# VectorE takes the low half of the turned units ahead of a coming tile's statistics

## The reference

```python
def _layernorm(x, axis=-1, eps=1e-05):
    m = jnp.mean(x, axis=axis, keepdims=True)
    v = jnp.var(x, axis=axis, keepdims=True)
    return (x - m) / jnp.sqrt(v + eps)

# cross attention, 8 heads of 128
q = (x @ Wq).reshape(B, Tq, h, C) * SCALE
k = (context @ Wk).reshape(B, Tk, h, C) * SCALE
v = (context @ Wv).reshape(B, Tk, h, C)
attn = jax.nn.softmax(jnp.einsum('bqhc,bkhc->bhqk', q, k), axis=-1)
out = jnp.einsum('bhqk,bkhc->bqhc', attn, v).reshape(B, Tq, h * C)
return out @ Wo + bo
...
# feed-forward: a shared expert, and routed ones whose weights are truncated
out_shared = _sq_relu(xf @ Ws1) @ Ws2
logits = xf @ Wr
...
prob = jnp.trunc(prob)
...
x = x + _L0_xattn_ref(_layernorm(x, axis=-1), ...)
x = x + _L0_ffn_ref(_layernorm(x, axis=-1), ...)
```

## Time and profile before

| what | value |
|---|---|
| median of 3 runs | 117.61 us (117.22 to 117.66) |
| profiled execution | 117.36 us |
| its span, first to last instruction | 115.5 us |
| granted TensorE clock, mean | 0.993 |
| TensorE matmuls busy | 109.2 us (95%), 854 instructions |
| VectorE busy | 87.8 us (76%), 350 instructions |
| ScalarE busy | 85.5 us (74%), 348 instructions |
| GpSimd busy | 65.5 us (57%), 106 instructions |

### The profile page before, as it was taken

How to read it: one execution, slowest core, us unless ns; L and a number is a source line. 1 busy time by engine, 2 the same in 40 slices (tenths; PEclk the granted TensorE clock), 3 DMA queues, 4 the chain that set the end, 5 groups by cost and what they waited for, 6 DMA issues and landing times.

```text
span 115.5 us, 3118 instructions
## 1 busy us (share of the span) xinstructions
PE 109.2 (95%) x854; PEld 105.9 (92%) x854; DVE 87.8 (76%) x350; ACT 85.5 (74%) x348; POOL 65.5 (57%) x106
## 2 busy tenths in 40 slices
PE   6976999999999999999999999999999999989981
PEld 6974999899998989999999999999999999979970
DVE  1009888569889697797979797797979696798963
ACT  4006925997948979898988889898988889994320
POOL 2005735855372965785676578657746865469250
PEclk9999999999999999999999999999999999999997
DMA  3799999994000200040005001300500050031032
GB/s 63 252 336 357 354 355 350 346 349 160 6 6 0 91 0 3 6 146 35 0 0 182 0 0 61 121 0 0 182 0 0 0 182 3 0 124 57 38 136 98
DMA packets 11815, 12.70 MB, mean 110 GB/s; under 512 B 1056, under 2 KB 10272, under 8 KB 11808
## 3 DMA queue, kind: packets, MB, share of 16 engines
q1 hardware_dynamic: 11520, 12.36, 32.4%
q10 hardware_dynamic: 288, 0.26, 0.7%
HBM read 8.42 MB, written 2.10 MB: 91 GB/s over the span
## 4 chain that ended last, share of the span: by engine, by line
PE 80%; DVE 7%; DMA 4%; ACT 2%; SPq 2%; issue 2%; POOL 1%; DVEq 0%; ACTq 0%
PE o_ps L435 8%; PE o_ps L437 8%; PE o_ps L436 8%; PE s_ps L435 7%; PE s_ps L437 7%; PE s_ps L436 7%; PE g_ps L493 6%; PE f_ps L523 4%; DMA wqt_sb<-in_wq_t 4%; PE g_ps L506 3%; PE f_ps L435 2%; PE g_ps L449 2%; ACT probs L712 1%; PE f_ps L437 1%; PE f_ps L436 1%
## 5 line engine op out<-in xcount | busy, mean ns | idle before, releaser
L712 ACT ACTIVATE probs<-s_ps,neg_max,rstd 128x77 f32<-128x77 f32 x112 | 45.2, 425 | 4.0 <-DVE neg_max L950 4.0
L840 POOL TENSOR_TENSOR probs<-probs,recip 128x308 f32<-128x308 f32 x27 | 18.9, 701 | 23.4 <-DVE recip L956 23.3
L712 ACT ACTIVATION_READ_ACCUMULATOR probs<-s_ps,neg_max,rstd 128x1 f32 x112 | 24.0, 214 | 0.0
L435 PE MATMUL o_ps<-u_hi,pt_hi 128*128 128x256 f32 (+1 forms) x80 | 22.7, 284 | 0.5 <-DVE pt_lo L964 0.5
L437 PE MATMUL o_ps<-u_lo,pt_hi 128*128 128x256 f32 (+1 forms) x80 | 22.4, 280 | 0.0
L436 PE MATMUL o_ps<-u_hi,pt_lo 128*128 128x256 f32 (+1 forms) x80 | 22.4, 280 | 0.0
L435 PE MATMUL s_ps<-a_hi,xt_hi 128*128 128x308 f32 x64 | 22.1, 345 | 0.0
L437 PE MATMUL s_ps<-a_lo,xt_hi 128*128 128x308 f32 x64 | 19.5, 304 | 0.0
L436 PE MATMUL s_ps<-a_hi,xt_lo 128*128 128x308 f32 x64 | 19.4, 303 | 0.0
L435 PEld LDWEIGHTS o_ps<-u_hi,pt_hi 128*128 128x128 f32 (+1 forms) x80 | 15.0, 188 | 0.9 <-DVE pt_lo L964 0.9
L436 PEld LDWEIGHTS o_ps<-u_hi,pt_lo 128*128 128x128 f32 (+1 forms) x80 | 15.1, 188 | 0.0
(11 more groups left out here) (188 smaller groups left out, 270.6 us busy)
## 6 DMA issues: line engine op xcount, KB each, us to landing
xt_sb<-in_x_t SPq DMA_DIRECT2D x8, 256.0 KB, 6.4
x_sb<-in_x SPq DMA_DIRECT2D x8, 256.0 KB, 6.3
x_sb<-x_tr SPq DMA_DIRECT2D x7, 256.0 KB, 2.3
out<-y_sb SPq DMA_DIRECT2D x6, 256.0 KB, 2.3
wqt_sb<-in_wq_t SPq DMA_DIRECT2D x4, 256.0 KB, 5.2
wo_sb<-in_wo SPq DMA_DIRECT2D x1, 1024.0 KB, 8.9
wk_sb<-in_wk_p SPq DMA_DIRECT2D x3, 256.0 KB, 3.2
wv_sb<-in_wv_p SPq DMA_DIRECT2D x2, 384.0 KB, 6.2
```

Of the source, the lines that this page charges most:

```text
L435: pe.matmul(out_ap, hi, rhs_hi, start=first, stop=False)
L712: e = act.activation(probs_of(t)[:, par, h * TK:(h + 1) * TK], s_ps[:, 2 * par + half, (h - half * H // 2) * TK:(h - half * H // 2 + 1) * TK],
L840: pool.tensor_tensor(rows, rows, recip[:, par, hs].unsqueeze(2).broadcast_to([P, H // 2, TK]), ALU.mult).then_inc(probs_ready, 1)
```

## The change

In `step` of VectorE the call of `lo_of_last` (L974) is put ahead of the call of `stats_x` (L914). The instructions are the same ones. In steps 12 and 13 the order stays as it was.

```diff
                 lo_of_transposes(t, par)
                 if live(t - 1, TILES):
                     stats_x1(t - 1, 1 - par)
+                lo_of_last(t, par)
                 if ahead:
                     stats_x(t + ahead, par)
-                lo_of_last(t, par)
                 if live(t - 1, TILES):
                     aggregate_x1(t - 1, 1 - par)
                 if ahead:
```

## The result

The kernel with the change takes 117.52 us (median of 22 runs, 117.08 to 118.15), the one before 117.10 us (22 runs beside them, 116.45 to 117.94). The ratio is 1.0039, with a 95% interval of 1.0024 to 1.0054: 0.4% slower, a small loss that the interval keeps clear of zero. The profiled execution took 117.77 us, 0.41 over that of before. That the forecast time of 117.5 lies on the median is luck: the three runs shown ahead were high. By its own sum the forecast was a difference of +0.02 us, no change, and +0.42 came. These 0.4 us are what has to be explained.

A forecast was written before the change was run, and what follows sets the result against it. Two cycles bound it: TensorE waiting for L974 (5.24 us a step) and the maxima's (5.19). L974's gain is eaten by the hold at L942: sum 117.38, 117.6 with the median's 0.25; forecast 117.5 us, range 116.7 to 118.0.

The forecast's parts named there:

- L974 earlier: VectorE's L974 moves up by 0.33 us, so TensorE waits less at L435; at most 0.96 us gained.
- The rival that ScalarE's L693 would hold L974: The 0.04 us margin to ScalarE's copy is gone, L974 comes no earlier, time stays at 117.6 us; chance 0.07.
- The hold by L914: VectorE's row maxima L942 wait for L914's end: 0.03 and 0.12 us in turn, 0.075 a step on average.
- The cycle that sets the pace: Row maxima, negation, ScalarE's exponentials and copy, VectorE's low half, next maxima: 5.19 us a step, 5.27 after the change.
- The leg "L942 to L950 0.93": On VectorE, from the row maxima to their negation, one leg of the maxima's cycle, read as 0.93 us in step 2.
- The round to step 12: From L968 of step 11 to L968 of step 12 on VectorE, forecast as 5.19+0.03, 5.22 us.
- The free wait: Rival: the wait ahead of L942 costs 0, or the maxima's cycle has more slack; 116.6 to 116.9 us, chance 0.22.
- The slower rival: Register work of two waits ahead of L942 makes it 0.21 us later each loop step; about 118.7 us, chance 0.11.

The follow-up runs named there:

- E9: Changed order, wait on `bn1_done` moved behind the maxima to L933, which now leads the four small instructions; 116.30 us, 0.9947 of the kernel before.
- E7: Changed kernel with VectorE's steps 2 to 11 written out, so its waits have constant targets; 117.05 us, 0.9998 of the kernel before.
- E10: Old order (L914 ahead of L974), wait on `bn1_done` moved behind the maxima to L933, now first of the small ones; 116.88 us, 0.9993 of the kernel before.
- E3: Changed order with L914 moved behind L950, its wait, L917 and L921 further down; 116.30 us, 0.993 of the kernel before.
- E1: Changed order with the wait for L914's end moved behind the row maxima, ahead of the reciprocals; 121.76 us, 1.0372 of the kernel before.
- E5: Changed order, wait for L914's end behind the row maxima, L917 and L921 moved behind L950; 121.42 us, 1.0373 of the kernel before.

## Why the prediction was right or wrong

- **L974 earlier: right.** It starts 61.62-60.68 = 0.94 after L968, before 61.85-60.58 = 1.27; TensorE gained 0.30 in step 2 (forecast 0.33) and ran ahead until the slower cycle had taken it back. The rival that ScalarE's L693 would hold L974 is out: L693 ends at 61.19, 0.43 ahead, a margin that grew as argued.
- **The hold by L914: right in both sizes.** L968 to L942 is 1.81 and 1.71 against 1.69: 0.12 and 0.02, where 0.12 and 0.03 were taken from L983 and L917. Against E9, where it is 61.72-60.04 = 1.68 without the hold, it is 0.13 and 0.03. E7 gives the split: 0.04 with constants in both steps.
- **The cycle that sets the pace: right.** E9 shows it without the hold: 5.19 on average, the value that the prediction had taken. It was a choice: the legs as it read them sum to 5.21, which is E9's even step (60.04 to 65.25); the odd steps last 5.16 to 5.17.
- **The leg "L942 to L950 0.93": this step failed.** The prediction priced a held instruction by its late start alone and kept its length. L942 lasts 0.80 where it starts 0.11 or more behind L929's start, and 0.77 where it starts 0.09 or less behind it. VectorE's L942, after and then before (count, ns of the shortest, the median, the longest):

```profile
L942 DVE TENSOR_REDUCE row_max<-s_ps x16: 767/799/800, 17.2 to 99.0; 128x8 f32<-128x616 f32 x16
```

```profile
L942 DVE TENSOR_REDUCE row_max<-s_ps x16: 764/767/800, 17.3 to 98.7; 128x8 f32<-128x616 f32 x16
```

  The median is 32 ns more, and what follows L942 comes later by as much: L942 to L950 takes 0.96 or 0.97 and 0.95 in turn, in E9 0.94 and 0.92. Nine rounds make 9x0.03 = 0.27 us. The trace of before had the row, in step 12, where L942 starts at L929's end (93.34+0.17 = 93.51):

```profile
93.34 0.17 DVE L929 BATCH_NORM_AGGREGATE mv<-bn 128x2 f32<-128x6 f32 x1
93.50 0.80 DVE L942 TENSOR_REDUCE row_max<-s_ps 128x8 f32<-128x616 f32 x1
```

- **Two small terms.** Five of the nine rounds, not half, start in an even step and pay the larger hold: (5x0.13+4x0.03)/9 = 0.086 on average instead of 0.075, so 9x0.011 = 0.10. The round to step 12 took 5.30 instead of 5.22: 0.03 by the longer L942 of step 11, the rest by L968 of step 12, which waited 0.38 instead of 0.31 (there, too, a second wait on `rstd1_done` stands ahead of it). Together 0.27+0.10+0.08 = 0.45 of the 0.47 us that the sum lacked.
- **Rivals.** The free wait is refuted: its mark was steps of 5.17, and they lasted 5.30. The sentence of the Trainium skill that would have made it free (VectorE: DVE Perf Modes, The DRAIN you can't avoid) is about a row of `tensor_copy` and does not carry over to this wait; the same section adds that "A next op that is not held starts earlier", and with that the rows agree. With the wait, L942 starts 0.21 and 0.11 after L929's start, and without it 0.08 (E9), at 0.9947 instead of 1.0039 times the kernel before. The slower rival had the right place and sign with the wrong price: the start was held by 0.12 and 0.02 in turn, not by 0.21.

What stays open: why L942 is longer when it starts later. That VectorE stands empty is not it: in the odd step L942 starts at 67.75, and L929 ends at 67.64+0.16 = 67.80, after it. In steps 1 to 13 of the kernels before and after and of E7 to E10 it lasts 0.80 when it starts over 0.1 us after L929's start, and 0.77 when it starts under 0.1 after. In E3 it lasts 0.80 too, without a wait on L914 ahead of it (61.18, L929 at 60.97), so it goes with the late start and not with that wait. No run changes its length alone: that the hold as a whole made the loss is shown (E9, E10), and its split into the late start and the longer run goes by rows. The kernel with the wait simply left out wasn't tried, since `bn1` would then be read without its order being secured.

## What to carry to other kernels

Where an instruction moves next to a wait on it, count what stood between as cover: L974 hid L914's end, and moving it cost more on one cycle than it freed on the other. When two cycles lie within 1% of each other, a change to the order must be priced on both, and a wait's price is the late start plus, as here, the longer run of what it holds. The wait can often follow the order: put it behind the critical instruction, ahead of the first reader of the data (E9), or move the producer behind the critical instructions (E3).

## What the runs showed of the hardware

- A VectorE instruction of 8 columns (L950) lasted 0.72 us instead of 0.23 when a GpSimd `tensor_tensor` (L840) started at the same moment (E1, E5), and ended with it; when it started 0.12 or 0.07 earlier, it lasted 0.23 (E9: 62.66 and 62.78; after: 63.45 and 63.52). The Trainium skill, SBUF — State Buffer, section SBUF: two separate sides, describes the port pair that VectorE and GpSimd share as an exclusive lock, between GpSimd and a VectorE instruction that runs in a 2-port mode or has two SBUF inputs: whichever starts first holds it for the whole instruction and "the other fully blocks". The rows agree that one waits out the other, at 0.49 us a step; which of the two started first they don't resolve, and no run shows which kind L950 is.
- In the loop, where the targets of waits are in registers, the hold of L942 was 0.13 and 0.04 us in turn; with the loop written out and constant targets it was 0.04 in both steps (E7).
- With the loop written out, a second wait ahead of L968 went with 0.06 us more (E7: 0.70 and 0.64 after L698). In the loop kernels both steps have 0.63 to 0.64, so the second wait alone is not shown to cost this.
